# A fused diffusion, expert and attention kernel: order inside the three-product sums, place of the turned maxima, and setup of the tiles

## The reference

```python
x = x + zX*lap_x(x) + zY*lap_y(x) + zR*x*(1 - x)          # diffusion, reflecting edges
g, u = h @ Wg[e], h @ Wu[e]                               # 8 gated experts and a shared one, F = 512
x = x + (1 - sg) * sum_e p[e] * (silu(g) * u) @ Wd[e] + sg * shared(x)
x = x + lora(x, language)                                 # rank 16, one of 4 languages
x = x + attention(q of side input, k and v of x and of the side input, 16 heads) @ Wo + bo
```

## Time and profile before

| | us |
|---|---|
| runs of the kernel before (3), lowest, median, highest | 445.8, 448.39, 448.97 |
| the profiled execution, whole | 448.04 |
| its span from first to last instruction | 446.3 |
| TensorE busy (share of the span) | 418.9 (94%) |
| VectorE, ScalarE, GpSimd busy | 318.1 (71%), 273.5 (61%), 164.6 (37%) |

### The profile page before, as it was taken

One profiled execution on the slowest core, in us unless ns is written; L12 is line 12 of the kernel. 1 busy time (PEld: TensorE's weight loads), 2 busy tenths in 40 slices (PEclk: granted clock), 3 DMA queues, 4 the chain that ended last, 5 costly groups with the idle time before them and its releaser, 6 DMA issues.

```text
span 446.3 us, 7157 instructions
## 1 busy us (share of the span) xinstructions
PE 418.9 (94%) x2318; PEld 329.1 (74%) x2318; DVE 318.1 (71%) x570; ACT 273.5 (61%) x517; POOL 164.6 (37%) x213
## 2 busy tenths in 40 slices
PE   8898699999999999999999999999999999886995
PEld 3676588887788877777888777878887775665673
DVE  3675857767667888767678888676688875666674
ACT  4677677776575655575765555655665558666582
POOL 2576647668222233232322333223263724112120
PEclk9999899999999999999999999999999999999899
DMA  5333234310034211000232110002493122525431
GB/s 166 120 98 96 71 85 157 109 29 0 1 98 120 72 49 51 1 27 0 94 101 68 53 50 2 26 0 90 113 282 114 44 71 84 173 82 164 137 92 29
DMA packets 50848, 35.92 MB, mean 80 GB/s; under 512 B 4952, under 2 KB 45308, under 8 KB 50812
## 3 DMA queue, kind: packets, MB, share of 16 engines
q1 hardware_dynamic: 50380, 35.37, 27.0%
q10 hardware_dynamic: 432, 0.10, 0.1%
HBM read 25.39 MB, written 10.00 MB: 79 GB/s over the span
## 4 chain that ended last, share of the span: by engine, by line
PE 79%; SPq 6%; DVE 5%; ACT 3%; issue 3%; DMA 3%; POOL 1%; ACTq 0%
PE acc_ps L556 7%; PE acc_ps L557 7%; PE u_ps L556 7%; PE acc_ps L558 7%; PE u_ps L558 7%; PE g_ps L556 7%; PE u_ps L557 7%; PE g_ps L558 7%; PE g_ps L557 7%; PE s_ps L619 3%; SPq L428 2%; PE g_ps L662 2%; DMA k_blk<-k_rows 2%; PE pv_ps L712 2%; SPq L409 2%
## 5 line engine op out<-in xcount | busy, mean ns | idle before, releaser
L821 ACT ACTIVATE act_hi<-u_ps 128x512 fp32r<-128x512 f32 x144 | 86.2, 598 | 89.7 <-DVE u_ps L1056 88.7
L1060 DVE TENSOR_TENSOR act_lo<-u_ps,act_hi 128x512 fp32r<-128x512 f32 x144 | 99.2, 689 | 52.0 <-ACT act_hi L821 48.7
L1056 DVE TENSOR_TENSOR u_ps<-act_p,u_ps 128x512 f32<-128x512 f32 x144 | 99.8, 693 | 33.0 <-ACT act_p L816 29.1
L816 ACT ACTIVATE act_p<-g_ps 128x512 f32<-128x512 f32 x144 | 86.1, 598 | 45.2 <-PE g_ps L558 45.0
L1218 POOL TENSOR_TENSOR xg_lo<-xg,xg_hi 128x512 fp32r<-128x512 f32 x35 | 45.7, 1305 | 136.9 <-ACT xg_hi L827 136.9
L556 PE MATMUL acc_ps<-act_hi,w_split 128*128 128x512 f32 x144 | 60.4, 419 | 2.8 <-DVE act_lo L1060 2.7
L556 PE MATMUL g_ps<-x_hi,w_split 128*128 128x512 f32 x144 | 56.4, 392 | 1.4 <-DVE x_lo L1084 1.4
L556 PE MATMUL u_ps<-xg_hi,w_split 128*128 128x512 f32 x144 | 56.3, 391 | 0.5 <-DVE xg_lo L1088 0.4
L557 PE MATMUL acc_ps<-act_lo,w_split 128*128 128x512 f32 x144 | 56.6, 393 | 0.0
L558 PE MATMUL acc_ps<-act_hi,w_split 128*128 128x512 f32 x144 | 56.3, 391 | 0.0
L558 PE MATMUL g_ps<-x_hi,w_split 128*128 128x512 f32 x144 | 56.2, 390 | 0.0
(11 more groups left out here) (153 smaller groups left out, 643.0 us busy)
## 6 DMA issues: line engine op xcount, KB each, us to landing
q_pl<-q_rows SPq DMA_DIRECT2D x16, 192.0 KB
k_blk<-k_rows SPq DMA_DIRECT2D x64, 48.0 KB
q_blocks<-q_rows SPq DMA_DIRECT2D x32, 96.0 KB
k_plain<-k_rows SPq DMA_DIRECT2D x8, 384.0 KB
w_raw<-in_L_cond_Wg SPq DMA_DIRECT2D x8, 256.0 KB, 2.9
w_raw<-in_L_cond_Wu SPq DMA_DIRECT2D x8, 256.0 KB, 2.7
w_raw<-in_L_cond_Wd SPq DMA_DIRECT2D x8, 256.0 KB, 3.0
q_rows<-rows_hi SPq DMA_DIRECT2D x8, 256.0 KB, 2.9
```

Source lines behind the costliest of these rows:

```text
L816: activation(act_p[m % 2][:], g_ps[m % 2][:], ACT.Silu).then_inc(silu_done, 1)
L821: activation(act_hi[m % 3][:], u_ps[m % 3][:], ACT.Identity).then_inc(act_hi_done, 1)
L1056: tt(u_ps[m % 3][:], act_p[m % 2][:], u_ps[m % 3][:], ALU.mult).then_inc(prod_done, 1)
L1060: tt(act_lo[m % 3][:], u_ps[m % 3][:], act_hi[m % 3][:].bitcast(F32), ALU.subtract).then_inc(act_lo_done, 1)
```

## The change

The edits, part by part:

- `three` puts the product with the low part of the moving operand last, and can take a semaphore that is awaited only ahead of that product. Gate, up and down products use it: they now start on the high part and await the low part ahead of the third product.
- `WARM_PRODUCTS` goes from 8 to 6.
- The first diffusion: the weighing moves from ACT to DVE (four TENSOR_SCALAR operations), `x_y` from POOL to ACT (four operations), DVE's parts run in the order 1, 0, 2, and POOL does not begin before `dif_ready`.
- `turn_max` stands between gate and up product instead of after the up product; ACT's copy stands ahead of its silu.
- "bias" and "setup" go from slots 6 and 9 to 5 and 8; the last three DVE operations of the bias step become `turn_bias`, one slot later, with a semaphore `cols_ready` of their own.
- For the later diffusions, the weighing on ACT goes to 7 slots ahead, the scaling to two halves 6 and 5 slots ahead (it was all scaling 5, weighing 4 ahead), and DVE's three parts go one slot earlier.

```diff
-WARM_PRODUCTS = 8
+WARM_PRODUCTS = 6
-SETUP_SLOT = {6: "bias", 9: "setup"}
+SETUP_SLOT = {5: "bias", 8: "setup"}
...
-            def three(dst, w_h, w_l, x_h, x_l, start=True, stop=True):
+            def three(dst, w_h, w_l, x_h, x_l, start=True, stop=True, low=None):
 
                 mm(dst, w_h, x_h, start=start, stop=False)
-                mm(dst, w_h, x_l, start=False, stop=False)
-                return mm(dst, w_l, x_h, start=False, stop=stop)
+                mm(dst, w_l, x_h, start=False, stop=False)
+                if low is not None:
+                    pe.wait_ge(low[0], low[1])
+                return mm(dst, w_h, x_l, start=False, stop=stop)
...
-                    pe.wait_ge(xg_ready, t * NE + e + 1)
+                    pe.wait_ge(xg_rounded, t * NE + e + 1)
...
-                pe.wait_ge(act_lo_done, m + 1)
+                pe.wait_ge(act_hi_done, m + 1)
                 three(acc_ps[:], w_hi[:, e, 2, chunk], w_lo[:, e, 2, chunk], act_hi[m % 3][:], act_lo[m % 3][:],
-                      start=(k == 0), stop=(k == SLOTS - 1)).then_inc(down_done, 1)
+                      start=(k == 0), stop=(k == SLOTS - 1), low=(act_lo_done, m + 1)).then_inc(down_done, 1)
...
-            pe.wait_ge(first_split, 1)
+            pe.wait_ge(aux_rounded, 1)
             gate_product(0, 0)
...
                     if t or k > 1:
                         gate_product(t, k)
-                    up_product(t, k)
                     turned = turn_at(t, k)
                     if turned is not None:
...
                         turn_max(turned, b * GI + i + 1, s_ps)
+                    up_product(t, k)
...
-            scale_x(0)
-            weigh_x(0)
+            scale_x(0, range(TB))
+            for b in range(TB):
+                last = activation(x_y[:, b], x_in[:, b], ACT.Identity, scale=z_all[:, 1, b:b + 1])
+            last.then_inc(y_ready, 1)
...
-                    silu(t, k)
                     turned = turn_at(t, k)
                     if turned is not None:
                         copy_max(turned, s_ps)
+                    silu(t, k)
...
+                    for kind, f, b in after_slot(t, k, 7):
+                        if kind == "diffuse":
+                            weigh_x(f)
+                    for kind, f, b in after_slot(t, k, 6):
+                        if kind == "diffuse":
+                            scale_x(f, range(0, TB // 2))
                     for kind, f, b in after_slot(t, k, 5):
                         if kind == "diffuse":
-                            scale_x(f)
-                    for kind, f, b in after_slot(t, k, 4):
-                        if kind == "diffuse":
-                            weigh_x(f)
+                            scale_x(f, range(TB // 2, TB))
...
-            for part in range(3):
-                diffuse_part(0, part)
+            dve.wait_ge(x_loaded, 16)
+            dve.wait_ge(z_ready, 2)
+            for b in range(TB):
+                ts(dif_b[:, b], x_in[:, b], z_less[:, b:b + 1], z_own[:, b:b + 1], ALU.mult, ALU.add).then_inc(x_weighted, 1)
+            diffuse_part(0, 1)
+            diffuse_part(0, 0)
+            diffuse_part(0, 2)
...
-                        for kind, f, b in after_slot(t, k, 3 - part):
+                        for kind, f, b in after_slot(t, k, 4 - part):
...
-            pool.wait_ge(z_loaded, 16)
-            scale_y(0)
+            pool.wait_ge(dif_ready, 1)
             split_part(0)
```

More of the change, by code:

```diff
@@ L285, in build @@
         in_lo_ready = sem("in_lo_ready")
-        cols_spread = sem("cols_spread")
+        cols_spread, cols_ready = sem("cols_spread"), sem("cols_ready")
         bias_done = sem("bias_done")
@@ L633, in gate_product @@
                 wait(pe, silu_done, m - 1)
-                three(g_ps[m % 2][:], w_hi[:, e, 0, chunk], w_lo[:, e, 0, chunk], x1_hi[t % 2][:], x1_lo[t % 2][:])\
-                    .then_inc(g_written, 1)
+                three(g_ps[m % 2][:], w_hi[:, e, 0, chunk], w_lo[:, e, 0, chunk], x1_hi[t % 2][:], x1_lo[t % 2][:],
+                      low=(first_split, 1)).then_inc(g_written, 1)
             def up_product(t, k):
@@ L642, in up_product @@
                         pe.wait_ge(w_lo_done, 3 * e + 2)
-                    pe.wait_ge(xg_ready, t * NE + e + 1)
+                    pe.wait_ge(xg_rounded, t * NE + e + 1)
                 wait(pe, act_lo_done, m - 2)
                 n = (t * NE + e) % 2
-                three(u_ps[m % 3][:], w_hi[:, e, 1, chunk], w_lo[:, e, 1, chunk], xg_hi[n][:], xg_lo[n][:]).then_inc(u_written, 1)
+                three(u_ps[m % 3][:], w_hi[:, e, 1, chunk], w_lo[:, e, 1, chunk], xg_hi[n][:], xg_lo[n][:],
+                      low=(xg_ready, t * NE + e + 1)).then_inc(u_written, 1)
             def down_product(m):
@@ L805, in aux_step @@
                 elif kind == "query":
+                    act.wait_ge(cols_ready, 1)
                     wait(act, rows_stored, 48 * 2 * f)
@@ L827, in round_xg, with scale_x @@
                 activation(xg_hi[n % 2][:], flat(xg), ACT.Identity).then_inc(xg_rounded, 1)
-            def scale_x(f):
+            def scale_x(f, batches):
                 act.wait_ge(x_loaded, 16 * (f + 1))
                 if f == 1:
-                    act.wait_ge(aux_drained, NTH["bias", 0, 0] + 1)
+                    act.wait_ge(cols_ready, 1)
                 elif f:
@@ L837, in scale_x @@
                         act.wait_ge(stored, 16 * TB * (f - 1) // 2)
-                for b in range(TB):
+                for b in batches:
                     activation(x_x[:, b, 1:D + 1], x_in[:, b], ACT.Identity, scale=z_all[:, 0, TB * f + b:TB * f + b + 1])\
                         .then_inc(x_scaled, 1)
-                act.wait_ge(x_scaled, TB * f + TB)
-                activation(x_x[:, :, 0:D + 2:D + 1], x_x[:, :, 2:D:D - 3], ACT.Identity).then_inc(x_padded, 1)
+                if batches[-1] == TB - 1:
+                    act.wait_ge(x_scaled, TB * f + TB)
+                    activation(x_x[:, :, 0:D + 2:D + 1], x_x[:, :, 2:D:D - 3], ACT.Identity).then_inc(x_padded, 1)
             def weigh_x(f):
+                act.wait_ge(x_loaded, 16 * (f + 1))
                 act.wait_ge(z_ready, 2)
-                wait(act, dif_ready, f)
+                act.wait_ge(dif_ready, f)
                 for b in range(TB):
@@ L1003, in aux_step @@
                     c = 0 if kind == "query" else 1
+                    dve.wait_ge(cols_ready, 1)
                     stt(rows_lo[:], aux_ps[:], cols[:, c:c + 1], rows_hi[:].bitcast(F32), ALU.add, ALU.subtract)\
@@ L1026, in aux_step, with turn_bias @@
                        bias_nat[:, 3].unsqueeze(1).to_broadcast([128, TB, D]), ALU.add).then_inc(aux_drained, 1)
+            def turn_bias():
+                dve.wait_ge(aux_drained, NTH["bias", 0, 0] + 1)
+                dve.wait_ge(bias_done, 3)
+                tt(b_diag[:, 0], bias_nat[:, 0], ident, ALU.mult).then_inc(bias_done, 1)
+                tt(b_diag[:, 1], bias_kp[:], ident, ALU.mult).then_inc(bias_done, 1)
+                dve.wait_ge(bias_done, 5)
+                nc.vector.tensor_reduce(cols[:, 0:2], b_diag, AX_X, ALU.add).then_inc(cols_ready, 1)
             def split_input(f):
@@ L1126, in _ @@
                             sum_self(f, b)
+                        if kind == "bias":
+                            turn_bias()
                     if m == 3:
```

7 lines of the change are left out of this document (1 added, 6 removed).

## The result

The changed kernel takes 436.62 us (median of 4 executions, 435.15 to 437.86); the kernel before takes 448.22 (445.8 to 448.97). The ratio is 0.9725 [0.9682, 0.9768]: 2.7% faster. The prediction was 435.5 with a range of 432 to 440. The profiled execution took 436.59, 11.45 less than that of before (448.04); its span is 434.8.

The account below looks back on a forecast made before the run. TensorE, busy 94% of the span, was taken to bound the kernel, so only its standstills could be won. Start 3.0, first tile 6.3 and turns 3.3 sum to 12.6 off 448.04, giving 435.5 us, range 432 to 440.

Parts of the forecast that it names:

- The start: Ahead of the first diffusion: DVE's new chain and fewer warm-ups start it at about 8.8 instead of 11.17, gaining 2.4 us.
- two products fewer put the last pass at 8.13 and its end at 8.6: Warm-up ahead of the first diffusion: passes 0.43 apart, so dropping two products lets the diffusion start at about 8.8.
- The low part last: First gate and up triples: only the third product waits for the low part, gaining 0.6 us (bounds 0 to 0.8).
- The first tile: Waits and half clock in the first tile: 8.3 us could go, 2.0 left standing, gain 6.3 (bounds 1.5 to 8.3).
- the half clock behind the wait: First tile, 53.00 to 56.30: lower clock level behind the diffusion's wait costs 1.65 us and should not come without it.
- The turns: Nine turned maxima: the score product's wait for ACT's copy, 6.0 us, goes; new waits take 2.7, gain 3.3.
- The new wait: At each of nine turns: the turn waits for DVE's maxima, still reading its bank; 0.3 us each, 2.7 in all.
- The tail: End of the kernel: standstills untouched, begins with the last down products and moves along; costed at nothing.
- The turn's wait (1): Rival: at the turns the new wait replaces the copy's wait, so they give 0; 438.7 us, chance 0.12.
- DVE blocked by POOL (2): Rival: in the first tile DVE stays blocked, the diffusion's wait (2.7) and half clock (1.65) stay; 439.7 us, chance 0.13.
- The clock (3): Rival: at the start, fewer warm-ups and a gate wait bring the lower clock, costing 1.65; 437.2 us, chance 0.07.
- A wait inside the triple (5): Rival: in 432 triples the wait delays loading the third product's weights, 0.08 each, 35 us lost; 470 us, chance 0.03.

Follow-up runs that it names:

- e7: Changed kernel with DVE's maxima moved ahead of the drain of the natural step in each slot; 433.89 us, ratio 0.9676.
- e1: Changed kernel with the low part's product second again in each triple and awaited ahead of the whole triple; 437.01 us, ratio 0.9739.
- e2: Changed kernel with the turn back behind the up product and ACT's copy back behind its silu; 440.29 us, ratio 0.9808.
- e4: Changed kernel with ACT's scaling and weighing and DVE's parts for the later diffusions back in their old slots; 439.78 us, ratio 0.9812.
- e5: Changed kernel with bias and setup back in slots 6 and 9 and the seven DVE bias operations in one row; 437.37 us, ratio 0.9755.
- e9: Changed kernel with DVE's part 1 of later diffusions six slots ahead, parts 0 and 2 three ahead, where POOL looked free; 436.20 us, ratio 0.9742.
- e12: One more execution of the changed kernel with the later diffusions' preparation in its old slots, run for its clock; 439.34 us.
- e3: Changed kernel with the first diffusion shared among ACT, DVE and POOL as before, and eight warm-up products; 437.40 us, ratio 0.9752.
- e8: Changed kernel with eight warm-up products instead of six, nothing else different; 436.54 us, ratio 0.9745.
- e11: One more execution of the unchanged kernel before, run for its clock; 446.21 us.
- e6: Changed kernel with three warm-up products instead of six, nothing else different; 437.38 us, ratio 0.975.
- e10: Changed kernel with the maxima first on DVE, the diffusion parts moved to where POOL looked free, and four warm-up products; 433.21 us, ratio 0.967.

## Why the prediction was right, point by point

**The start** was the step that failed in part: 1.45 instead of 2.4 at the diffusion. The chain on DVE was right (ready at 8.68, forecast 8.7; four TENSOR_SCALARs 1.12, estimated 1.0). What failed is "two products fewer put the last pass at 8.13 and its end at 8.6": I took the last passes of one execution, 0.43 apart, as the pace of all. In the profiled execution of after they stood 0.85 apart until 7.57 and ended at 9.72. e7, with the same start, has its diffusion at 8.79 and the second up triple at 14.55, the 8.8 and 14.5 that I had named. Eight profiled executions have this start with six products (after, e1, e2, e4, e5, e7, e9, e12): their diffusion begins at 8.73 to 9.72, 9.20 on the mean. So the step holds in some executions and in others loses up to 0.9. In e3, e8 and e7 the passes came to 0.43 apart at nearly the same time (4.86, 4.83 and 5.01), and so they divide the 2.4: the chain on DVE is worth 11.19 - 9.98 = 1.2, the two products 9.98 - 8.79 = 1.2.

**The low part last**: 0.59 between diffusion and second up triple, forecast 0.6, and e1 shows about the same. That it stays won until the second tile was wrong: 0.3 of it does.

**The first tile**: 6.1, forecast 6.3. The edits alone: preparation of the diffusion 3.4 (e4, e12), bias step 1.3 (e5), order 0.3 (e1). These come to 5.0 of the 6.70 between diffusion and second tile. The other 1.7 is the half clock behind the wait, 1.64 in before's profiled execution by the difference of that slot to e11's. It was costed at the right size (1.65), but as a property of the kernel, and e11 shows that it can be missing. That 6.1 came out beside 6.3 is in that part luck: the profiled execution of before happened to have the stretch, and that of after had none there. Measured against e11, the changed kernel gains 446.21 - 436.59 = 9.6 instead of 11.45. How often before has the stretch isn't known: of its 21 other executions beside the experiments three have the mean granted clock of e11, 0.999, and the rest, at 0.982 to 0.995, spent more time at half clock in places that aren't on record.

**The turns**: 3.7, forecast 3.3. The new wait is there with the cause and size that I had given, 0.31 for the first two turns of a tile (0.3 forecast) and 0.10 for the third. e2 shows that the turn alone makes this difference, e7 that the maxima are what it waits for. Another 0.2 came from the two diffusion slots of the later tiles (3.84 instead of 3.95 each), which I had at nothing; 0.1 is scatter.

**The tail** was put at 0 and took 0.73 more. It varies between 79.1 and 82.5 among kernels whose tail is the same program save the order in its triples, with stretches at half clock in different places (0.54 from 399.50 to 407.00 above). No edit is aimed at it, and e2, e3 and e8 have 79.1 to 79.3, as before has; whether the change makes such stretches likelier isn't shown. The spread is as large as most single parts.

**The rivals.** The turn's wait (1) took 2.3 of the 6.0 and not all. DVE blocked by POOL (2) is seen: two parts take 1.70 and 1.68 where 0.69 is their length alone. By the letter that is a sign I had named for being wrong (the third part runs over 1.5 and ends behind TensorE), but one slot more of lead covers most of it: 0.33 of wait is left. The Trainium skill (SBUF — State Buffer, "two separate sides") has this as an exclusive lock of the port pair; the trace agrees: the three lengthened parts shown here (39.44 and 44.27 in after, 34.53 in e9) end at 41.14, 45.95 and 35.85, each 0.55 behind the end of the POOL operation that had begun before them (40.59, 45.40 and 35.30), whatever their own start. The clock (3) didn't fall in the start: 12.35 follows a wait of 0.69, and the stretch from 16.70 is at 1.00. A wait inside the triple (5) costs nothing where it is met: in 422 of the 432 triples the third product stands 0.22 to 0.24 behind the second; the other ten, all in the first tile, have 0.28 to 0.58, 1.4 us over that pace in all.

**The sum** came out 1.15 too high: 0.95 at the start and 0.73 in the tail against the prediction, 0.2 in the first tile as well, 0.73 in the later tiles for it. The second tile begins 8.15 earlier and not the 9 that I had named, for the same reasons. A slip in the chances: 0.97 less 0.06 is 0.91 and not 0.90.

## What to carry to other kernels

Where a wait on the bottleneck engine has been moved, look at once for the instruction that it now waits for and at what stands ahead of that on its own engine: here a reorder of two steps on DVE was worth another 2 us. What one execution's timeline shows of a start need not be the pace of all. Preparation that meets another engine's work needs a lead longer than its durations alone add up to: a slot more of it removed most of the wait here, while a place that looked free only moved it. And a stretch at half clock in one profile is a property of that execution until a second one shows it.

## What I had not expected of the hardware

- The passes of the warm-up came to their full pace at very different times at the same program start: 0.85 apart until 7.57 in after, 0.43 apart from 5.01 in e7. The view of stretches shows the granted clock at 1.00 there in both, so it can't be read from that. But the trace has a first record at full clock at 7.51 in after and at 4.95 in e7, just ahead of the first pass that stands 0.43 from the next (7.57 and 5.01); so I read 0.85, twice 0.43, as the distance at the lower of the two levels. Over the 14 profiled executions that first record stands between 4.60 and 7.51. The Trainium skill (TensorE: Matmul & The Clock Gate, Part 1) says that the moment of this change varies from run to run, and by 0.5 us either way; the traces agree on the first and show about three times as much, a span of 2.9.
- A standstill of TensorE of 2.5 to 3.0 us (four executions, two kernels) was followed by half clock once. No run here tells what decided it.
- A late start was not made up in any of these runs: from the diffusion to the second tile seven kernels with the same first tile (after, e2, e3, e6, e7, e8 and, but for its moved parts, e10) take 85.05 to 85.39, whether the diffusion starts at 8.65 or at 11.19.
